# Adapter rows in column quarters, second-layer adapters through SyncE, image chunks one tile later

## The chip, the cores and the metric

One core of one Trainium2 chip runs the kernel. The metric is device time in microseconds, the median over runs of one build. TensorE is called PE here, as in the profile.

## What is computed

Two layers with a residual each, over eight sequences of 512 tokens and 2048 features, in float32. The first adds a rank-16 product, the second adds a dense product, a bias and a second rank-16 product. Which adapter (A, B pair) a sequence uses comes from two vectors of eight integers.

```python
def L0(x, A, B, ids):                       # scale 16/16 = 1
    Bx = einsum('bni,bri->bnr', x, B[ids])
    return einsum('bnr,bor->bno', Bx, A[ids])
def L1(x, ids, W, b, lora_As, lora_Bs):     # scale 32/16 = 2
    base = einsum('bti,oi->bto', x, W) + b
    h = einsum('bti,bir->btr', x, lora_As[ids])
    return base + 2 * einsum('btr,bro->bto', h, lora_Bs[ids])
x = x + L0(x, L0_A, L0_B, ids0)
x = x + L1(x, ids1, W, b, lora_As, lora_Bs)
```

## The kernel before

The dense product of 2048 by 2048 weights with two sequences at a time is cut as one level of Strassen-Winograd style blocking: `GROUPS` = 4 pairs of sequences, `PRODUCTS` = 7 block products per pair, and eight output tiles of 128 features per product. One (group, product, tile) is a **step**; there are 224, numbered `s`, and every engine walks them in the same order. A step multiplies eight 128x128 weight tiles with 128x512 tokens, each product as three matmuls of float32r halves (hi by hi, lo by hi, hi by lo; L502 to L504), so 24 matmuls. For each step SyncE (SP) loads a block of W (`w_one`, 512 KB), for products that need a sum or difference of two blocks a second (`w_two`), VectorE (DVE) sums them (L639), SP stores the sum to memory for the later groups (`w_sums`, L290), ScalarE (ACT) makes the hi half (L537), DVE the lo half (L643). A product's four pairs of x tiles go the same way (L656 or L659, L555, L665). `w_one` has three buffers, and a load into one waits until the store of its last sum has landed (L272).

Beside this runs the **background**: chunks `z`, each a 128x1024 piece that is loaded (SP, L317), split by ACT (`bg_hi`, L565) and DVE (`bg_lo`, L670) and multiplied on PE between the matmuls of a step. Chunks 0 to 31 are the **image chunks**: they carry W (`w_rows`) through the first layer's up matrices A of all eight sequences at once (L454 to L456, six matmuls a chunk), eight chunks to one column quarter j of 512 columns in `image_ps`. The last matmul of a quarter, L462, adds the two layers' rank-by-rank product (`across`) times the second layer's up rows `b1_rows`; DVE then adds the first layer's rows `a0_rows` (L781) and SP stores the quarter (L377). The finished images, one of 16 rows per sequence, are what both rank products need later. `background(s)` names the chunks of a step: steps 1 to 16 have two each. `bg_raw`, `bg_hi` and `bg_lo` have two buffers, so the load of chunk z waits until DVE has split chunk z-2, and the split of z until PE has used z-2. The SP queue is strictly in order: what stands behind such a wait waits too.

`across` needs the second layer's down matrices of all sequences (`a1_raw`), which ACT copies into contiguous columns (L607), and 16 matmuls in plain float32 (L521), which the profile counts as 32. They stand on PE between step 1 and step 2.

GpSimd (POOL) issues all loads whose address depends on an adapter number: it reads the number into a register and issues a DMA, for `a0_raw` (8 of 128 KB, L424), then `a1_raw` (8 of 128 KB, L427), then the rows: `load_rows(half)` issues 16 DMAs of 16 rows by 1024 columns (64 KB each, L415 and L417) into one buffer per table. The second half waits until quarters 0 and 1 are finished (`image_ready` 2), because it overwrites the first. Both PE (L461) and DVE (L778) wait for the whole half. Behind the rows stand POOL's loads for the later background (L392, L394) and for the ranks (L405, L407).

```python
for half in range(2):
    load_rows(half)
for s in range(STEPS):
    ...
```

## Time and profile before

| what | value |
|---|---|
| median of 3 runs | 1414.97 us (1413.96 to 1415.28) |
| the profiled execution | 1417.38 us |
| its span in the trace | 1415.7 us |
| PE busy | 1373.6 us, 97% |
| DVE busy | 939.9 us, 66% |
| ACT busy | 486.1 us, 34% |
| bytes moved by DMA | 308.38 MB, mean 218 GB/s |
| mean granted TensorE clock | 0.99 of full speed |

The page divides the span in 40 slices of 35 us. PE is at nine tenths or more in all but the first and the fifth (its digits are `3999799...`), and the granted clock dips at both places. So the question for any change is what PE waits for in the first 190 us, and the views to read are the waits by engine in a stretch of time, and the timelines of PE, POOL, ACT and DVE there. A row of a timeline gives start, duration, engine, line and shapes, with the idle time before it in brackets and what ended it.

### The profile page before, as it was taken

What the parts mean: (1) busy time and instruction counts of PE and PEld (TensorE: products, weight loads), DVE (VectorE), ACT (ScalarE), POOL (GpSimd) and SP (SyncE); (2) the same over time, 40 slices, a digit from 0 to 9 for tenths busy, and PEclk for the clock granted to TensorE, in tenths of its full rate; (3) what the DMA queues carried; (4) which work ended last, traced back from release to release, by engine and by line L of the source; (5) the groups of instructions that cost most, each with busy time, mean ns of one, the idle gap of its engine ahead of it and who ended that gap; (6) DMA issues with size and microseconds to landing.
All of it is one profiled execution on the core that took longest, in us unless ns stands there. A gap on an engine that the chain in (4) does not pass through costs nothing.

```text
span 1415.7 us, 15911 instructions
## 1 busy us (share of the span) xinstructions
PE 1373.6 (97%) x5992; PEld 1129.5 (80%) x5992; DVE 939.9 (66%) x991; ACT 486.1 (34%) x491; POOL 80.6 (6%) x166
## 2 busy tenths in 40 slices
PE   3999799999999999999999999999999999999999
PEld 2788587888887888888888888888888888888887
DVE  6587568887866665757666666566756756666662
ACT  3343244333323343433233333332223334332331
POOL 2202001001001000000101000000101000000000
PEclk8899899999999999999999999999999999999999
DMA  9999766999897444566757444556866444457642
GB/s 361 294 334 348 249 225 204 349 342 345 280 341 247 135 140 142 168 207 218 252 193 228 148 134 134 175 183 215 270 211 197 163 154 134 145 164 251 201 153 82
DMA packets 101100, 308.38 MB, mean 218 GB/s; under 512 B 13344, under 2 KB 13472, under 8 KB 101024
## 3 DMA queue, kind: packets, MB, share of 16 engines
q1 hardware_dynamic: 95328, 294.77, 62.0%
q0 software_dynamic: 5696, 12.59, 2.9%
q8 instruction: 48, 0.79, 0.2%
q14 instruction: 28, 0.23, 0.0%
HBM read 251.73 MB, written 55.57 MB: 217 GB/s over the span
## 4 chain that ended last, share of the span: by engine, by line
PE 93%; issue 3%; DMA 1%; DVE 1%; POOLq 1%; POOL 0%; ACT 0%; ACTq 0%
PE acc L502 28%; PE acc L503 28%; PE acc L504 28%; PE acc L486 2%; PE down_ps L472 2%; PE down_ps L473 2%; POOLq L386 1%; PE image_ps L456 1%; PE image_ps L455 1%; PE image_ps L454 1%; PE down_ps L521 0%; DMA a_raw<-a 0%; DMA ids_sb<-ids 0%; DMA b_rows<-b 0%; PE image_ps L462 0%
## 5 line engine op out<-in xcount | busy, mean ns | idle before, releaser
L502 PE MATMUL acc<-x_hi,w_hi 128*128 128x512 f32 x1792 | 703.6, 393 | 17.0 <-DVE x_lo L665 16.3
L503 PE MATMUL acc<-x_lo,w_hi 128*128 128x512 f32 x1792 | 699.9, 391 | 0.0
L504 PE MATMUL acc<-x_hi,w_lo 128*128 128x512 f32 x1792 | 699.3, 390 | 0.0
L537 ACT ACTIVATE w_hi<-w_one 128x1024 fp32r<-128x1024 f32 x224 | 237.5, 1060 | 679.3 <-PE acc L504 644.3
L502 PEld LDWEIGHTS acc<-x_hi,w_hi 128*128 128x128 f32 x1792 | 338.1, 189 | 91.0 <-issue 16.4
L503 PEld LDWEIGHTS acc<-x_lo,w_hi 128*128 128x128 f32 x1792 | 338.2, 189 | 72.1 <-issue 1.2
L504 PEld LDWEIGHTS acc<-x_hi,w_lo 128*128 128x128 f32 x1792 | 337.7, 188 | 71.4
L643 DVE TENSOR_TENSOR w_lo<-w_one,w_hi 128x1024 fp32r<-128x1024 f32 x224 | 273.6, 1222 | 104.2 <-ACT w_hi L537 103.9
L665 DVE TENSOR_TENSOR x_lo<-x_stage,x_hi 128x1024 fp32r<-128x1024 f32 x80 | 96.1, 1221 | 42.8 <-ACT x_hi L555 42.8
L708 DVE SCALAR_TENSOR_TENSOR sums<-acc,bias_sb,sums 128x512 f32<-128x512 f32 x128 | 95.7, 748 | 39.0 <-PE acc L486 39.0
L555 ACT ACTIVATE x_hi<-x_stage 128x1024 fp32r<-128x1024 f32 x80 | 83.5, 1056 | 110.3 <-DVE x_stage L659 82.9
L670 DVE TENSOR_TENSOR bg_lo<-bg_raw,bg_hi 128x1024 fp32r<-128x1024 f32 x64 | 77.7, 1221 | 30.5 <-ACT bg_hi L565 30.2
L565 ACT ACTIVATE bg_hi<-bg_raw 128x1024 fp32r<-128x1024 f32 x64 | 67.1, 1052 | 64.9 <-DMA bg_raw<-w_rows 35.5
L659 DVE TENSOR_TENSOR x_stage<-x_stage,resident 128x1024 f32<-128x1024 f32 x64 | 78.0, 1218 | 3.1 <-DMA x_stage<-x 3.1
L405 POOL DMA_DIRECT2D rank_raw<-images x48 | 23.4, 487 | 872.8 <-issue 872.8
L690 DVE TENSOR_TENSOR sums<-sums,acc 128x512 f32<-128x512 f32 x32 | 21.9, 685 | 64.5 <-PE acc L504 64.5
L639 DVE TENSOR_TENSOR w_one<-w_one,w_two 128x1024 f32<-128x1024 f32 x40 | 48.7, 1219 | 11.2 <-DMA w_two<-w 11.2
L472 PE MATMUL down_ps<-bg_hi,down 128*128 128x512 f32 x128 | 50.2, 392 | 1.8 <-issue 1.2
L486 PE MATMUL acc<-rank_x,rank_w 96*128 96x512 f32 x128 | 50.8, 397 | 0.0
L473 PE MATMUL down_ps<-bg_lo,down 128*128 128x512 f32 x128 | 49.8, 389 | 0.0
L687 DVE TENSOR_TENSOR sums<-sums,acc 128x512 f32<-128x512 f32 x32 | 21.9, 684 | 39.4 <-PE acc L504 39.3
L693 DVE TENSOR_TENSOR sums<-sums,acc 128x512 f32<-128x512 f32 x32 | 22.0, 686 | 39.0 <-PE acc L504 39.0
(54 smaller groups left out, 622.0 us busy)
## 6 DMA issues: line engine op xcount, KB each, us to landing
w_one<-w_sums SPq DMA_DIRECT2D x120, 512.0 KB, 3.3
w_one<-w SPq DMA_DIRECT2D x104, 512.0 KB, 5.5
x_stage<-x SPq DMA_DIRECT2D x64, 512.0 KB, 4.3
out<-sums SPq DMA_DIRECT2D x128, 256.0 KB, 4.5
w_two<-w SPq DMA_DIRECT2D x40, 512.0 KB, 8.1
w_sums<-w_one SPq DMA_DIRECT2D x40, 512.0 KB, 6.4
resident<-x SPq DMA_DIRECT2D x32, 512.0 KB, 7.4
bg_raw<-w_rows SPq DMA_DIRECT2D x32, 512.0 KB, 5.8
```

Source lines behind the costliest of these rows:

```text
L472: pe.matmul(down_ps[:, :], weights, hi[:, u, :], start=(c == 0), stop=False)
L473: mm = pe.matmul(down_ps[:, :], weights, lo[:, u, :], start=False, stop=(c == C - 1))
L486: pe.matmul(acc[s % BANKS][:, :], rank_w[:, P * o:P * (o + 1)], rank_x[side][:, :], start=False, stop=True, skip_group_check=True).then_in ...
L502: pe.matmul(ps[:, :], w_hi[ws][:, c, :], hi, start=(c == 0), stop=False)
L503: pe.matmul(ps[:, :], w_hi[ws][:, c, :], lo, start=False, stop=False)
L504: mm = pe.matmul(ps[:, :], w_lo[ws][:, c, :], hi, start=False, stop=(c == H - 1))
L537: act.activation(w_hi[s % W_PARTS][:, :, :], w_one[s % W_ONES][:, :, :], ACT.Copy).then_inc(w_hi_ready, 1)
L555: act.activation(x_hi[q % X_PARTS][:, :, :], x_source(p, r), ACT.Copy).then_inc(x_hi_ready, 1)
L643: dve.tensor_tensor(w_lo[s % W_PARTS][:, :, :], w_one[s % W_ONES][:, :, :], f32(w_hi[s % W_PARTS][:, :, :]), ALU.subtract).then_inc(w_read ...
L659: dve.tensor_tensor(stage, stage, resident[1 if i in (2, 6) else 0][:, cs, :], ALU.subtract if i in (1, 6) else ALU.add).then_inc(x_summed, 1)
L665: dve.tensor_tensor(x_lo[q % X_PARTS][:, :, :], x_source(p, r), f32(x_hi[q % X_PARTS][:, :, :]), ALU.subtract).then_inc(x_ready, 1)
L708: dve.scalar_tensor_tensor(out=tile, in0=acc[s % BANKS][:, :], scalar=bias_sb[:, f:f + 1], in1=tile, op0=ALU.add, op1=ALU.add).then_inc(ba ...
```

## The change

- The rows come by quarter: `load_rows(j)` for j = 0 to 3 issues 16 DMAs of 16 rows by 512 columns (32 KB each), `b1` ahead of `a0`, into buffer j % 2 with a semaphore of its own. Quarters 2 and 3 wait for quarter 0 and 1 (`image_ready` 1 and 2). There are 64 such DMAs in place of 32, with the same bytes.
- The eight `a1_raw` loads leave POOL. SP reads the numbers and issues them, behind the loads for step 2 and ahead of `mask`, `bias` and the first store of a sum.
- Image chunks begin in step 2, not 1: two a step, three in steps 11 and 14, the last still in step 16. Chunks 0 and 1 go from ahead of `across` to behind it on PE, ACT, DVE and SP.
- DVE makes the first lo half of x before the second sum of x, not after it.

On PE, before: the end of step 1 (`acc` is the dense product, `image_ps` the image, `down_ps` here the matmuls of `across`).

```order
L504 MATMUL acc<-x_hi,w_lo 128x512
L454 MATMUL image_ps<-bg_hi,a_hi 128x512
L455 MATMUL image_ps<-bg_hi,a_lo 128x512
L456 MATMUL image_ps<-bg_lo,a_hi 128x512
L454 MATMUL image_ps<-bg_hi,a_hi 128x512
L455 MATMUL image_ps<-bg_hi,a_lo 128x512
L456 MATMUL image_ps<-bg_lo,a_hi 128x512
L502 MATMUL acc<-x_hi,w_hi 128x512
L503 MATMUL acc<-x_lo,w_hi 128x512
L504 MATMUL acc<-x_hi,w_lo 128x512
L502 MATMUL acc<-x_hi,w_hi 128x512
L503 MATMUL acc<-x_lo,w_hi 128x512
```

And after, from the end of step 1 on:

```order
L507 MATMUL acc<-x_lo,w_hi 128x512
L508 MATMUL acc<-x_hi,w_lo 128x512
L527 MATMUL down_ps<-a_raw,sums 128x128 x16
L506 MATMUL acc<-x_hi,w_hi 128x512
L507 MATMUL acc<-x_lo,w_hi 128x512
L508 MATMUL acc<-x_hi,w_lo 128x512
L506 MATMUL acc<-x_hi,w_hi 128x512
L507 MATMUL acc<-x_lo,w_hi 128x512
L508 MATMUL acc<-x_hi,w_lo 128x512
L458 MATMUL image_ps<-bg_hi,a_hi 128x512
L459 MATMUL image_ps<-bg_hi,a_lo 128x512
L460 MATMUL image_ps<-bg_lo,a_hi 128x512
```

Step 1 now has no image matmul in it; the first stands behind `across` and six matmuls of step 2.

On SP, before: the start of the queue.

```order
L296 DMA resident<-x 128x1024 x8
L279 DMA w_one<-w 128x1024
L284 DMA w_two<-w 128x1024
L317 DMA bg_raw<-w_rows 128x1024 x2
L279 DMA w_one<-w 128x1024
L284 DMA w_two<-w 128x1024 [waits w_summed]
L352 DMA mask_sb<-mask 128x128
L353 DMA bias_sb<-bias 128x16
L290 DMA w_sums<-w_one 128x1024 [waits w_summed] x2
L279 DMA w_one<-w 128x1024 [waits w_kept0,w_ready]
L284 DMA w_two<-w 128x1024 [waits w_summed]
L306 DMA x_stage<-x 128x1024 [waits x_ready]
```

And after, in two places:

```order
L280 DMA w_one<-w 128x1024
L285 DMA w_two<-w 128x1024 [waits w_summed]
L346 TENSOR_LOAD ids_sb [waits ids_loaded]
L346 ISA x2
L357 ISA
L357 DMA a_raw<-a 128x256
```

```order
L359 DMA mask_sb<-mask 128x128
L360 DMA bias_sb<-bias 128x16
L291 DMA w_sums<-w_one 128x1024 [waits w_summed] x2
L280 DMA w_one<-w 128x1024 [waits w_kept0,w_ready]
L285 DMA w_two<-w 128x1024 [waits w_summed]
L307 DMA x_stage<-x 128x1024 [waits x_ready]
L318 DMA bg_raw<-w_rows 128x1024 x2
```

The first two chunk loads (1 MB) left the place ahead of step 2's weights and stand behind step 3's; the eight adapter loads (1 MB) came in behind step 2's weights.

```diff
--- before.py
+++ after.py
@@ -69,8 +69,9 @@
     if g:
         places = (0, 2, 4, 5)
         return [IMAGE + 16 * g + 4 * i + places.index(o)] if i < 4 and o in places else []
-    if 1 <= s <= 16:
-        return [2 * s - 2, 2 * s - 1]
+    if 2 <= s <= 16:
+        first = 2 * (s - 2) + (s > 11) + (s > 14)
+        return list(range(first, first + (3 if s in (11, 14) else 2)))
     if 19 <= s <= 22:
         return [IMAGE + 2 * (s - 19), IMAGE + 2 * (s - 19) + 1]
     return [IMAGE + 8 + s - 24] if 24 <= s <= 31 else []
@@ -165,8 +166,8 @@
             sb("first_tiles", [P, 2, T], F32, early)
             a0_hi = sb("a0_hi", [P, C, NB, R], F32R, early)
             a0_lo = sb("a0_lo", [P, C, NB, R], F32R, early)
-            a0_rows = sb("a0_rows", [P, D // 2], F32, early)
-            b1_rows = sb("b1_rows", [P, D // 2], F32, early)
+            a0_rows = [sb(f"a0_rows{k}", [P, T], F32, early) for k in range(2)]
+            b1_rows = [sb(f"b1_rows{k}", [P, T], F32, early) for k in range(2)]
             image = sb("image", [P, T], F32, early)
             mask_sb = sb("mask_sb", [P, P], F32, early)
             across = sb("across", [P, P], F32, early)
@@ -194,7 +195,7 @@
         a0_loaded = sem("a0_loaded")
         a1_loaded = sem("a1_loaded")
         mask_loaded = sem("mask_loaded")
-        rows_loaded = sem("rows_loaded")
+        rows_loaded = [sem(f"rows_loaded{k}") for k in range(2)]
         a1_ready = sem("a1_ready")
         across_done = sem("across_done")
         across_ready = sem("across_ready")
@@ -341,14 +342,20 @@
                 sp.dma_start(out[C * (2 * g + side) + H * half + o], sums[(2, 1, 2, 0)[i - 3]][:, o, :])\
                   .then_inc(out_stored[o], DMA)
 
+            def adapter(n, table):
+                a = sp.value_load(ids_sb[0:1, 1, n:n + 1], min_val=0, max_val=table.shape[0] - 1)
+                return table[bass.ds(a, 1)]
+
             load_w(0)
             for r in range(CH):
                 for k in range(2):
                     load_resident(0, k, r)
             load_w(1)
-            for z in background(1):
-                load_bg(z)
             load_w(2)
+            sp.wait_ge(ids_loaded, 2 * DMA)
+            for n in range(NB):
+                sp.dma_start(a1_raw[:, n, :, :], adapter(n, a1).rearrange("u p c r -> (u p) c r"))\
+                  .then_inc(a1_loaded, DMA)
             sp.dma_start(mask_sb[:, :], mask).then_inc(mask_loaded, DMA)
             sp.dma_start(bias_sb[:, :], bias).then_inc(bias_loaded, DMA)
             keep_sum(0)
@@ -406,16 +413,16 @@
                         .then_inc(rank_loaded, DMA)
                     pool.dma_start(rank_raw[row + R:row + 2 * R, :], up).then_inc(rank_loaded, DMA)
 
-            def load_rows(half):
-                if half:
-                    pool.wait_ge(image_ready, 2)
-                cols = slice(D // 2 * half, D // 2 * (half + 1))
+            def load_rows(j):
+                if j >= 2:
+                    pool.wait_ge(image_ready, j - 1)
+                cols = slice(T * j, T * (j + 1))
                 for n in range(NB):
                     rows = slice(R * n, R * (n + 1))
-                    pool.dma_start(a0_rows[rows, :], adapter(0, n, a0).rearrange("u r d -> (u r) d")[:, cols])\
-                        .then_inc(rows_loaded, DMA)
-                    pool.dma_start(b1_rows[rows, :], adapter(1, n, b1).rearrange("u r d -> (u r) d")[:, cols])\
-                        .then_inc(rows_loaded, DMA)
+                    pool.dma_start(b1_rows[j % 2][rows, :], adapter(1, n, b1).rearrange("u r d -> (u r) d")[:, cols])\
+                        .then_inc(rows_loaded[j % 2], DMA)
+                    pool.dma_start(a0_rows[j % 2][rows, :], adapter(0, n, a0).rearrange("u r d -> (u r) d")[:, cols])\
+                        .then_inc(rows_loaded[j % 2], DMA)
 
             pool.dma_start(ids_sb[:, 0, :], ids0).then_inc(ids_loaded, DMA)
             pool.dma_start(ids_sb[:, 1, :], ids1).then_inc(ids_loaded, DMA)
@@ -423,11 +430,8 @@
             for n in range(NB):
                 pool.dma_start(a0_raw[:, n, :, :], adapter(0, n, a0_down).rearrange("u p c r -> (u p) c r"))\
                     .then_inc(a0_loaded, DMA)
-            for n in range(NB):
-                pool.dma_start(a1_raw[:, n, :, :], adapter(1, n, a1).rearrange("u p c r -> (u p) c r"))\
-                    .then_inc(a1_loaded, DMA)
-            for half in range(2):
-                load_rows(half)
+            for j in range(4):
+                load_rows(j)
             for s in range(STEPS):
                 g, i, o = where(s)
                 if s + 4 in FIRST:
@@ -458,8 +462,8 @@
                     if k == 7:
 
                         pe.wait_ge(across_ready, 1)
-                        pe.wait_ge(rows_loaded, 2 * NB * DMA * (j // 2 + 1))
-                        pe.matmul(ps[:, :], across[:, :], b1_rows[:, T * (j % 2):T * (j % 2 + 1)],
+                        pe.wait_ge(rows_loaded[j % 2], 2 * NB * DMA * (j // 2 + 1))
+                        pe.matmul(ps[:, :], across[:, :], b1_rows[j % 2][:, :],
                                   start=False, stop=True).then_inc(image_done, 1)
                     return
                 if k == 0:
@@ -512,6 +516,8 @@
                         add_rank(s - 1)
                     if c == 5 and len(zs) > 1:
                         multiply_chunk(zs[1])
+                    if c == 6 and len(zs) > 2:
+                        multiply_chunk(zs[2])
 
             step(0)
             step(1)
@@ -601,8 +607,6 @@
             act.wait_ge(a0_loaded, NB * DMA)
             act.activation(a0_hi[:, :, :, :], a0_raw[:, :, :, :].rearrange("p n c r -> p c n r"), ACT.Copy)\
                .then_inc(a0_hi_ready, 1)
-            for z in background(1):
-                split_bg(z)
             act.wait_ge(a1_loaded, NB * DMA)
             act.activation(a1_cols.rearrange("p (c n r) -> p c n r", c=C, n=NB),
                            a1_raw[:, :, :, :].rearrange("p n c r -> p c n r"), ACT.Copy).then_inc(a1_ready, 1)
@@ -732,8 +736,8 @@
             sum_w(0)
             sum_x(0, 0)
             split_w(0)
+            split_x(0, 0)
             sum_x(0, 1)
-            split_x(0, 0)
             sum_x(0, 2)
             split_x(0, 1)
             sum_x(0, 3)
@@ -746,8 +750,6 @@
             dve.tensor_tensor(a0_lo[:, :, :, :], a0_raw[:, :, :, :].rearrange("p n c r -> p c n r"),
                               f32(a0_hi[:, :, :, :]), ALU.subtract).then_inc(a0_ready, 1)
             sum_w(2)
-            for z in background(1):
-                split_bg(z)
             for s in range(STEPS):
                 g, i, o = where(s)
                 p = PRODUCTS * g + i
@@ -775,11 +777,11 @@
                 if s - 1 in IMAGE_LAST:
                     j = IMAGE_LAST[s - 1]
                     dve.wait_ge(image_done, j + 1)
-                    dve.wait_ge(rows_loaded, 2 * NB * DMA * (j // 2 + 1))
+                    dve.wait_ge(rows_loaded[j % 2], 2 * NB * DMA * (j // 2 + 1))
                     if j:
                         dve.wait_ge(image_stored, DMA * j)
-                    dve.tensor_tensor(image[:, :], image_ps[j % 2][:, :], a0_rows[:, T * (j % 2):T * (j % 2 + 1)],
-                                      ALU.add).then_inc(image_ready, 1)
+                    dve.tensor_tensor(image[:, :], image_ps[j % 2][:, :], a0_rows[j % 2][:, :], ALU.add)\
+                       .then_inc(image_ready, 1)
                 if s - 1 in LAST:
                     split_rank_x(LAST[s - 1])
                 if s + 1 in FIRST:
```

## Rows read from the trace of the kernel before

**Rows 1.** The page: its first line and the busy time of PE.

```profile
span 1415.7 us, 15911 instructions
...
PE 1373.6 (97%) x5992; PEld 1129.5 (80%) x5992; DVE 939.9 (66%) x991; ACT 486.1 (34%) x491; POOL 80.6 (6%) x166
```

**Rows 2.** Busy time by stretch: stretch, length, PE, PEld, DVE, ACT, POOL, clock, DMA share, GB/s.

```profile
240.00:1416.00 1176.00, 1170.11 (x5141) 964.81 (x5139) 778.24 (x829) 392.21 (x398) 49.82 (x102) 1.00 0.61 203
...
154.00:155.00 1.00, 1.00 (x3) 0.35 (x2) 0.00 (x0) 0.00 (x0) 0.00 (x0) 0.50 0.94 307
```

**Rows 3.** Waits from 0 to 60 us: engine and line, releaser, total us, times, longest.

```profile
PE down_ps L521 <- ACT sums L607: 3.3, 1, 3.3
...
DVE x_stage L656 <- DMA resident<-x: 4.0, 4, 1.7
```

**Rows 4.** Waits from 60 to 240 us.

```profile
PE image_ps L462 <- DMA b_rows<-b: 10.6, 1, 10.6
```

**Rows 5.** Timeline of PE, steps 1 and 2.

```profile
25.84 0.50 PE L502 MATMUL acc<-x_hi,w_hi 128*128 128x512 f32 x1
...
33.53 0.80 PE L454 MATMUL image_ps<-bg_hi,a_hi 128*128 128x512 f32 x1 [6.04 <-DVE bg_lo L670]
...
46.12 6.56 PE L521 MATMUL down_ps<-a_raw,sums 128*128 128x128 f32 x32 [3.33 <-ACT sums L607]
...
52.43 0.48 PE L502 MATMUL acc<-x_hi,w_hi 128*128 128x512 f32 x1
```

**Rows 6.** Timeline of POOL and ACT in the first 50 us.

```profile
26.97 1.91 ACT L602 ACTIVATE a_hi<-a_raw 128x2048 fp32r<-128x2048 f32 x1 [2.45 <-DMA a_raw<-a_down]
...
37.73 0.54 POOL L427 DMA_DIRECT2D a_raw<-a  x1 [6.14 <-issue]
...
44.07 1.91 ACT L607 ACTIVATE sums<-a_raw 128x2048 f32<-128x2048 f32 x1 [13.29 <-DMA a_raw<-a]
```

**Rows 7.** Timeline of the SP queue, first 31 us.

```profile
10.27 4.33 SPq L353 DMA_DIRECT2D bias_sb<-bias  x1
...
30.20 0.43 SPq L306 DMA_DIRECT2D x_stage<-x  x1
```

**Rows 8.** DMA issues from 0 to 60 us: KB each, us to landing.

```profile
bias_sb<-bias SPq DMA_DIRECT2D x1, 8.0 KB, 17.9
```

**Rows 9.** Timeline of POOL, the second half of the rows.

```profile
122.69 0.49 POOL L415 DMA_DIRECT2D a_rows<-a  x1 [64.32 <-issue]
...
148.68 0.48 POOL L417 DMA_DIRECT2D b_rows<-b  x1 [6.94 <-issue]
```

**Rows 10.** Timeline of PE around the long wait.

```profile
153.54 2.04 PE L462 MATMUL image_ps<-b_rows,across 128*128 128x512 f32 x2 [10.58 <-DMA b_rows<-b]
...
157.83 0.40 PE L502 MATMUL acc<-x_hi,w_hi 128*128 128x512 f32 x1
```

**Rows 11.** Timeline of DVE and PE: chunks 4, 6, 8, 20, 22; PE uses 20.

```profile
58.45 1.22 DVE L670 TENSOR_TENSOR bg_lo<-bg_raw,bg_hi 128x1024 fp32r<-128x1024 f32 x1
...
66.11 1.23 DVE L670 TENSOR_TENSOR bg_lo<-bg_raw,bg_hi 128x1024 fp32r<-128x1024 f32 x1 [0.50 <-ACT bg_hi L565]
...
76.97 2.35 DVE L670 TENSOR_TENSOR bg_lo<-bg_raw,bg_hi 128x1024 fp32r<-128x1024 f32 x2
...
127.75 2.35 DVE L670 TENSOR_TENSOR bg_lo<-bg_raw,bg_hi 128x1024 fp32r<-128x1024 f32 x2
...
129.18 0.39 PE L454 MATMUL image_ps<-bg_hi,a_hi 128*128 128x512 f32 x1
...
135.64 1.23 DVE L670 TENSOR_TENSOR bg_lo<-bg_raw,bg_hi 128x1024 fp32r<-128x1024 f32 x1 [1.77 <-ACT bg_hi L565]
```

**Rows 12.** DMA from 52 to 142 us: SP's queue, chunk loads.

```profile
q1 hardware_dynamic: 8128, 29.09, 93.0%
...
bg_raw<-w_rows SPq DMA_DIRECT2D x20, 512.0 KB, 5.9
```

**Rows 13.** Timeline of PE, the first matmul of step 17.

```profile
191.41 0.39 PE L502 MATMUL acc<-x_hi,w_hi 128*128 128x512 f32 x1
```

## What the change does to the time: the prediction

> **What bounds the kernel now.** I read the page first. PE is busy 1373.6 of 1415.7 us [rows 1]; only 42 us are left to any change that keeps the matmuls, as this one does. The busy time by stretch says where: from 240 us to the end PE works 1170.11 of 1176 us at full clock [rows 2]. So the end of the kernel is set by PE, and whatever PE wins before 240 us comes through whole, if the later stage keeps its relative order. The change touches nothing after step 17, except that POOL's loads come earlier. From that stretch I also take PE's pace: 1170.11 us / 5141 matmuls = 0.228 us each; below I use 0.227.
>
> Next I read the waits of PE and the timelines around them. There are two places. The first is steps 1 and 2. Step 1 starts at 25.84, does six matmuls, then stands 6.04 us for the lo half of chunk 0 [rows 5]. After the step PE waits 3.3 us more for ACT's copy of the second layer's matrices [rows 3], does the 32 pieces of `across` in 6.3 us (46.12 to 52.43) and starts step 2 at 52.43 [rows 5]. The cause of the 3.3 stands on POOL and ACT: the last adapter load of the second layer is issued at 37.73 after a hole of 6.14 us, and ACT waits 13.29 us until 44.07 [rows 6]. The second place is the long wait: PE stands 10.58 us, until 153.54, for the rows of the second half [rows 4, 10]. POOL could begin them only at 122.69, when quarter 1 was finished, and issues one every 1.14 us or so; the sixteenth fell on a hole of 6.94 us and left at 148.68 [rows 9].
>
> **The sum, part by part.** All times are of the profiled execution (1417.38 us; 2.4 above the median 1414.97).
>
> *Chunks 0 and 1 out of step 1.* Step 1 still starts at 25.84, since what released it is w_lo, which is not moved. Its 24 matmuls then run through: 25.84 + 24 x 0.227 = 31.3.
>
> *Adapters on SP.* In SP's queue, in order, 8.4 MB stand ahead of the last adapter load: weights and x for steps 0 to 2 (7.3 MB) and the adapters themselves (1.05 MB). Before, exactly as much stood ahead of `bias`, with two chunk loads in the adapters' place. It was issued at 10.27 and landed 17.9 us later, at 28.2 [rows 7, 8]. So I put the adapters' landing at 28.2. SP's eight register reads and issues, at POOL's 1.14 us, take until 18 us, which the queue's backlog hides. The 4.33 us that `bias` took to issue [rows 7] says SP was held back by a full queue anyway. ACT finishes the first layer's split at 26.97 + 1.91 = 28.9 [rows 6] and copies the second's until 30.8, ahead of 31.3. The 3.3 us wait is gone.
>
> *`across` itself.* It took 6.3 us at, nearly throughout, the lower clock, because PE had just stood. Now PE comes from step 1 without a hole. No row shows it at the higher clock. Bounds: 6.3 us, and half of it, 3.2; I take 3.7, near the low end, since the dense matmuls go from 0.427 to 0.227 when the clock rises. Step 2 starts at 31.3 + 3.7 = 35.0. It started at 52.43 with 12 chunk matmuls already done, which now follow: 12 x 0.227 = 2.7. **Gain 52.4 - 35.0 - 2.7 = 14.7 us** (12.1 with the slow `across`).
>
> *The rows by quarter.* Quarter 2 needs only quarter 0's buffer. POOL can issue its 16 DMAs at some 80 us, 18 us of issuing, one hole of 7 and 5 of landing: ready by 110, while PE asks for it in step 13, near 137. Quarter 3: released near 112, ready by 142, asked for near 160. So the 10.58 us wait goes, and with it the lower clock behind it (0.50 at 154 us, [rows 2]). Between 153.54 and 157.83 PE does L462 (two pieces) and six matmuls in 4.3 us; at full clock they take 2.2. **Gain 10.6 + 2.1 = 12.7 us.** The 32 extra issues cost POOL 36 us. I cost them at nothing: POOL's next work, the loads for chunk 32 on, is needed after step 17. Without that cover they would cost their length past it.
>
> *First lo half of x earlier.* PE starts some 1.4 us earlier, but the later pairs wait for the loads of x [rows 3], which do not move. Between 0 and 1.4 us I take 0, as the last pair decides.
>
> Sum so far: 27.4 us. The block of steps up to the end of step 16 would end at 191.4 [rows 13] - 27.4 = 164.0.
>
> *What is late next: the chunks.* They are now asked for 15 to 27 us earlier, and the last 14 in six steps. Three prices. (1) Chunk 0 is loaded behind step 3's first x_stage, at 30.20 + 0.43 [rows 7] = 30.6; with 5.9 us to landing [rows 12], ACT 1.06 and DVE 1.22, it is ready at 38.9, and PE wants it at 35.0 + 6 x 0.227 = 36.4: 2.5 us of waiting, 0 to 2.1 more if the clock falls (the excess of [rows 10]); 3.5. (2) Before, DMA was already full from 52 to 142 us (SP's queue alone held 93% of the engines' time, [rows 12]), and the chunks lost their lead: from chunk 4 to chunk 22 DVE's start went from 58.45 to 135.64, 8.58 us a pair, where PE takes 36 x 0.227 = 8.2. Chunk 20's lo half was done only some 0.3 us before its use (127.75 + 1.22, used 129.18, [rows 11]). With no lead to start from, 0.4 a pair over eight pairs is 3 us. (3) In steps 11 to 16 PE asks for a pair every 7.7 us. At 8.58 that is 0.9 x 7 = 6 more; but half of these steps have light weight traffic, so the chunks can come faster: 1 to 2. Sum 8, of bounds 1 (the queue gains what PE gives it) and 12. Check from the other end: 38.9 + 15.5 pairs x 8.58 = 171.9, and 3.6 us of matmuls behind the last chunk: 175.5, so 11.5 late is the full price of a chain that never catches up.
>
> **Forecast: 27.4 - 8 = 19.4, with rounding 20 us**, 1397.4 in a profiled execution, 1395 as a median.
>
> **Rivals.**
> - *Full gain.* Chunks arrive faster because DMA has no gap before step 2 any more. For it: the engines' share falls when PE is slow, so capacity is left there. Against: the shrinking lead of [rows 11]. Only price (1) at its least: saves 26, 1389. Chance 0.16.
> - *Adapters late on SP.* One queue in order is slower for them than POOL's own. For it: loads of the same time landed 17.9 us after issue on SP [rows 8], and eight reads and issues stand ahead of the sum's store, for which step 3's weights wait. If they land 6 us later than 28.2, PE stands 5 us, the clock falls, `across` takes 6.3: step 2 starts near 42.5, and chunk 0's wait is covered. Saves 27.4 - 7.5 - 4.5 = 15, 1400. Chance 0.18. The Trainium skill (DMA: Bandwidth & Descriptors, "Queues, rings and completion order") says each DMA engine goes round-robin between the queues it has work for, packet by packet, and consumes one queue in order; by that rule a load moved from POOL's queue behind SP's backlog loses its turn, which speaks for this rival. The trace agrees with the rule so far (POOL's last adapter load, issued at 37.73, was in by 44.07, [rows 6], beside SP's 17.9), but the bytes ahead say 28.2.
> - *Three chunks starve.* In steps 11 and 14 the third chunk needs its buffer, freed only in the step before, and SP stands behind that wait, so the weights of two steps on are late too. Each costs 3 to 5 us with the clock's fall: 8 on top, saves 11.5, 1403.5. For it: chunk 20's 0.3 us. Chance 0.12.
> - *A hole remains.* POOL's holes fall elsewhere and a quarter is still late, or the change does not remove the long wait: saves 14.7 less 7, 1407. Against: 27 us of margin for quarter 2, 18 for quarter 3. Chance 0.03.
> - *Slower.* The chain load, ACT, DVE becomes PE's bound over the whole block because 64 small DMAs and the adapters disturb it. Place: steps 2 to 16. Price: the slowest pair before took 10.9 us (66.11 to 76.97, [rows 11]). At that pace the block ends at 38.9 + 15.5 x 10.9 + 3.6 = 211.5, 20 us later than now: 1435. It decides from 191.4 = 42.5 + 15.5p, p = 9.6 us a pair. Against: the mean is 8.58. Chance 0.03. The Trainium skill (same page, the section "Measured (HBM→SBUF, 128 partitions, SWDGE, issued from GpSimd)") calls transfers under 64 KB descriptor-dominated, and the row loads go from 64 to 32 KB; it would speak for this rival, but they are 2.1 MB in all.
>
> **How the numbers follow.** The forecast has 0.48: 1391 to 1399. I can tell from no change about 0.2%, 2.8 us. Every case but the last is faster by more: 0.95 faster, 0.02 the same, 0.03 slower. The range takes in full gain (1388) and the starved steps (1405).
>
> **What would show it.** In the trace after: step 2's first matmul near 35; `across` in some 3.7 us at clock 1.0; no wait at L466 of microseconds; adapters' copy starting at 28.9; a wait of 2 to 3 us for chunk 0; short waits of PE for `bg_lo` in steps 9 to 15; step 17 starting near 172. A copy that starts past 31 makes the second rival right, PE never waiting for `bg_lo` the first. If PE after 240 us is less than 99% busy, my premise that the rest is untouched is wrong.

## The result, and the profile after

| | before | after |
|---|---|---|
| median of 8 runs each | 1413.95 us (1412.76 to 1415.54) | 1409.57 us (1405.57 to 1411.68) |
| profiled execution, its span | 1417.38, 1415.7 us | 1411.09, 1409.2 us |

The ratio is 0.9962, with a 95% interval of 0.9951 to 0.9973: faster by 5.4 us of 1415 (4.4 by the medians), where 20 were forecast. 1409.57 lies outside the range of the prediction, on its slow side.

The page of the kernel after: span, busy times, the shares by engine of the chain that ends last, and the cost of making the chunks' hi halves on ACT.

```profile
span 1409.2 us, 16105 instructions
PE 1374.2 (98%) x5992; PEld 1127.3 (80%) x5992; DVE 940.1 (67%) x991; ACT 485.7 (34%) x491; POOL 91.7 (7%) x190
...
PE 84%; DMA 7%; DVE 4%; SPq 2%; ACT 1%; issue 1%; DVEq 0%; ACTq 0%
...
L571 ACT ACTIVATE bg_hi<-bg_raw 128x1024 fp32r<-128x1024 f32 x64 | 67.3, 1054 | 82.8 <-DMA bg_raw<-w_rows 72.3
```

PE does the same work as in [rows 1]. The other two lines tell where to look. The chain that sets the end was 93% PE in the page of before; here it is 84%, and 7% is DMA. ACT's idle time ahead of `bg_hi` that a chunk's load ended was 35.5 us and is 72.3.

Busy time of the kernel after by stretch (columns as in [rows 2]): the late stage, two stretches of the chunk stage, and the five microseconds behind chunk 0.

```profile
240.00:1409.00 1169.00, 1164.81 (x5121) 961.52 (x5119) 772.46 (x823) 390.67 (x396) 46.91 (x96) 1.00 0.61 203
41.00:46.00 5.00, 4.94 (x12) 3.88 (x13) 4.36 (x6) 1.56 (x2) 1.94 (x4) 0.50 1.04 354
60.00:152.00 92.00, 84.15 (x358) 66.32 (x357) 69.18 (x68) 35.18 (x35) 16.23 (x34) 1.00 0.93 325
152.00:186.00 34.00, 31.75 (x129) 24.90 (x128) 18.52 (x19) 12.16 (x12) 1.38 (x3) 0.95 0.70 226
```

After 240 us PE is busy 99.6% of the time, as in [rows 2]: the late stage is untouched. Between 60 and 152 us PE now stands 8 of 92 us; the kernel before was busy 82.00 of 82.00 from 60 to 142. From 152 to 186 it loses time and some of the clock (0.95).

The timeline of PE in the kernel after, at the places of [rows 5], and its start of step 17.

```profile
31.76 3.73 PE L527 MATMUL down_ps<-a_raw,sums 128*128 128x128 f32 x32
35.25 0.48 PE L506 MATMUL acc<-x_hi,w_hi 128*128 128x512 f32 x1
...
41.06 0.79 PE L458 MATMUL image_ps<-bg_hi,a_hi 128*128 128x512 f32 x1 [4.20 <-DVE bg_lo L674]
...
185.80 0.39 PE L506 MATMUL acc<-x_hi,w_hi 128*128 128x512 f32 x1
```

Step 1 (from 26.26) runs through, `across` stands behind it without a wait and takes 3.73 us, step 2 starts at 35.25, where it started at 52.43. Of that only 5.6 us are left when step 17 starts (185.80, [rows 13] had 191.41). The waits of PE from 60 to 240 us:

```profile
PE image_ps L458 <- DVE bg_lo L674: 10.0, 8, 2.4
...
PE acc L506 <- DVE w_lo L647: 0.5, 1, 0.5
```

The one long wait for the rows [rows 4] has gone, and eight short ones for a chunk's lo half came. DVE waited for ACT there, and ACT for the load:

```profile
ACT bg_hi L571 <- DMA bg_raw<-w_rows: 59.9, 25, 7.7
DVE bg_lo L674 <- ACT bg_hi L571: 31.1, 20, 4.7
```

Putting the first image matmul of some chunks side by side shows the pattern (us; the step in brackets):

| chunk | before | after |
|---|---|---|
| 2 | 53.91 (2) | 51.89 (3) |
| 8 | 79.31 (5) | 78.96 (6) |
| 15 | 107.87 (8) | 107.52 (9) |
| 23 | 141.45 (12) | 146.61 (13) |
| 31 | 187.80 (16) | 182.18 (16) |

At chunk 8 and at chunk 15 both kernels are at the same absolute time. What the change won shows only as one more step (24 dense matmuls, 5.5 us) done beside them. The 28.6 us between these two chunks are PE's own pace in both (126 matmuls of 0.227), so what the kernel after loses in the first half it loses ahead of chunk 8. From chunk 16 on the kernel after is slower than the chunks' old pace. So two theories stood against each other.

- **Supply**: the chain load, ACT, DVE for the chunks, through SP's queue in order and two buffers, is what sets the time of this stage, whatever PE wins ahead of it.
- **Arrangement**: the loss is made by something the change itself put there: chunk 0 loaded late, three chunks in steps 11 and 14, or the adapters in SP's queue.

### The profile page after: what moved, and what is told of

It is laid out like the page before. It is cut to its first block, busy times and chain, and to the rows that moved or that the text cites. A ratio compares the mean times of both kernels' runs of the same rounds, so it can differ in the third digit from the quotient of the medians.

```text
span 1409.2 us, 16105 instructions
## 1 busy us (share of the span) xinstructions
PE 1374.2 (98%) x5992; PEld 1127.3 (80%) x5992; DVE 940.1 (67%) x991; ACT 485.7 (34%) x491; POOL 91.7 (7%) x190
## 4 chain that ended last, share of the span: by engine, by line
PE 84%; DMA 7%; DVE 4%; SPq 2%; ACT 1%; issue 1%; DVEq 0%; ACTq 0%
PE acc L506 26%; PE acc L507 26%; PE acc L508 26%; DMA bg_raw<-w_rows 6%; PE down_ps L476 2%; PE acc L490 2%; PE down_ps L477 2%; DVE bg_lo L674 1%; ACT bg_hi L571 1%; DMA w_two<-w 1%; DVE w_one L643 1%; DMA w_sums<-w_one 1%; SPq L357 0%; DVE w_lo L647 0%; SPq L297 0%
## 5 line engine op out<-in xcount | busy, mean ns | idle before, releaser
L571 ACT ACTIVATE bg_hi<-bg_raw 128x1024 fp32r<-128x1024 f32 x64 | 67.3, 1054 | 82.8 <-DMA bg_raw<-w_rows 72.3
L697 DVE TENSOR_TENSOR sums<-sums,acc 128x512 f32<-128x512 f32 x32 | 22.0, 686 | 38.9 <-PE acc L508 38.9
```

Of the source, the lines that this page charges most:

```text
L571: act.activation(bg_hi[z % 2][:, :, :], bg_source(z), ACT.Copy).then_inc(bg_hi_ready, 1)
```

## The experiments

Every ratio below is to the kernel before in the same session, whose median was 1415.2 to 1415.9 us there. `A` marks an edit to the kernel after, `B` one to the kernel before. "Version 2" is the kernel of experiment 2, and so on. The expectations call some of them by other names: e1 is experiment 1, e2 is 3, e3 is 6, e7 is 2.

### 1. Two chunks a step (A)

```diff
-    if 2 <= s <= 16:
-        first = 2 * (s - 2) + (s > 11) + (s > 14)
-        return list(range(first, first + (3 if s in (11, 14) else 2)))
+    if 2 <= s <= 17:
+        return [2 * (s - 2), 2 * (s - 2) + 1]
```

> The changed kernel with two image chunks in every step from 2 to 17, none with three; the last quarter is finished one step later. Theory A (the steps with three chunks are at fault: SP stands behind the third chunk's wait and the next steps' weights and chunks are late): of the 11.4 us that chunks 18 to 31 came late, 8 to 11 are saved, so some 1400 us, and PE's waits for the lo halves after chunk 18 nearly vanish. Theory B (the DMA engines are simply full and every byte has its price): the same bytes must arrive before the same work, so 1408 to 1411, with the waits spread evenly over the steps. Theory C (the last quarter finished later pushes the rank work): a new wait of PE around step 24, 1412 or more.

Measured: 1409.63 us, ratio 0.9961 (0.9947 to 0.9974): nothing gained on the median. Yet the trace shows chunk 31 at 177.76, in step 17. Less the 5.5 us of one more step's dense matmuls that is 172.3, 9.9 us ahead of the kernel after. That is Theory A's 8 to 11 us. Part of it was lost again right behind. The SP queue of this kernel, and PE at step 19:

```profile
166.73 0.43 SPq L279 DMA_DIRECT2D w_one<-w  x1
180.17 0.33 SPq L327 DMA_DIRECT2D sums<-x  x1
180.54 0.43 SPq L279 DMA_DIRECT2D w_one<-w  x1
181.02 0.90 SPq L317 DMA_DIRECT2D bg_raw<-x  x2
```

```profile
191.99 0.47 PE L475 MATMUL down_ps<-bg_hi,down 128*128 128x512 f32 x1 [3.64 <-DVE down L717]
```

SP issues nothing for 13 us: the load of x into `sums` for step 18 waits until the fourth quarter is finished, which now happens a step later. I had not seen this wait. SP stands there in the kernels before and after too (11 to 12 us), but PE waits for nothing behind it: from step 18 to step 24 both take 40.0 us, this version 43.8, version 2 of the next experiment 40.6. In the trace this version is still 6.1 us ahead of the kernel after at step 24 (225.21 to 231.29). The profiled execution (1406.82) was the fastest of six, up to 1411.97, and why the median kept none of the 6 us no run shows.

### 2. The same, with that load behind the chunk loads of the next iteration (A)

```diff
-                if s + 2 < STEPS:
-                    load_sum(s + 2)
+                for t in {16: [], 17: [18, 19]}.get(s, [s + 2]):
+                    if t < STEPS:
+                        load_sum(t)
```

> Two chunks a step in steps 2 to 17, and SP's load of the running sum of step 18 moved behind the chunk loads of the next iteration, so that SP does not stand until the last quarter is done. In e1 that stand delayed chunks 32 and 33 and with them PE by 3.6 us and 2 us of lower clock. If e1 had won step 17's dense work and lost it there: 5 us below e1, 1402 to 1405. If the supply of chunks gives no gain from more room: 1408 to 1410.

Measured: 1402.37 us, ratio 0.9910 (0.9892 to 0.9928), chunk 31 at 177.87. That is in the range of the first case. This version is 7.4 us ahead of the kernel after (0.9962 less 0.9910, of 1415). The late load of `sums` only takes back the stand of experiment 1; in the kernel after PE lost nothing to it. What three chunks in a step do is plain in the two SP queues. After:

```profile
114.05 9.60 SPq L318 DMA_DIRECT2D bg_raw<-w_rows  x3
123.69 0.43 SPq L291 DMA_DIRECT2D w_sums<-w_one  x1
...
146.58 9.48 SPq L318 DMA_DIRECT2D bg_raw<-w_rows  x3
```

And with two a step:

```profile
112.93 2.19 SPq L317 DMA_DIRECT2D bg_raw<-w_rows  x2
115.17 0.43 SPq L290 DMA_DIRECT2D w_sums<-w_one  x1
115.69 0.38 SPq L279 DMA_DIRECT2D w_one<-w  x1
116.11 0.89 SPq L284 DMA_DIRECT2D w_two<-w  x1
```

The third load needs the buffer of the first, which DVE splits only in its next iteration (two splits from 122.07 on); SP stands until 123.65, and the store of a sum, the weights and the next chunks stand behind it. The busy time by stretch, 119 to 124 us, after and with two a step:

```profile
119.00:124.00 5.00, 4.19 (x19) 3.17 (x18) 4.21 (x4) 2.88 (x3) 0.00 (x0) 1.00 0.11 44
```

```profile
119.00:124.00 5.00, 4.10 (x18) 3.11 (x17) 5.00 (x6) 3.04 (x3) 0.00 (x0) 1.00 0.92 342
```

The DMA engines run nearly empty (a share of 0.11, 44 GB/s) in the stage that lives on them; with two a step it is 0.92 and 342 GB/s. No run kept three chunks in a step and moved the third load alone, so the runs show what 15 steps in place of 16 cost, and the traces show the stand. At chunk 23, between the two steps with three, version 2 is 5.1 us ahead (144.19, less half a step's 2.7, to 146.61), at chunk 31 9.8: each such step cost some 5 us.

### 3. Chunks 0 and 1 loaded earlier (A)

The two loads go from behind step 3's weights to directly behind the adapters, ahead of `mask` (20.28 us in place of 31.41).

```diff
                   .then_inc(a1_loaded, DMA)
+            for z in background(2):
+                load_bg(z)
             sp.dma_start(mask_sb[:, :], mask).then_inc(mask_loaded, DMA)
...
-                for z in background(s + 2):
-                    load_bg(z)
+                if s:
+                    for z in background(s + 2):
+                        load_bg(z)
```

> The changed kernel with the loads of chunks 0 and 1 issued behind the adapters and ahead of the mask, not behind step 3's weights. If chunk 0's late load is a cost of its own, the 4.2 us wait at 41 us and the 2.4 us of lower clock behind it go: 1402 to 1404 us. If the chain of chunks is bound by DMA throughput from there on, the lateness only moves to the next chunks: 1408 to 1410 us.

Measured: 1409.34 us, 0.9956 (0.9943 to 0.9968), not to be told from the kernel after, as in the second case of the expectation. Chunk 0's first matmul is at 41.02, where it was at 41.06. DVE tells why:

```profile
38.60 1.23 DVE L646 TENSOR_TENSOR w_one<-w_one,w_two 128x1024 f32<-128x1024 f32 x1 [3.61 <-DMA w_two<-w]
39.75 2.35 DVE L677 TENSOR_TENSOR bg_lo<-bg_raw,bg_hi 128x1024 fp32r<-128x1024 f32 x2
```

The data was there, but the split stands in DVE's order behind the sum of step 3's weights, whose load came 3 us later now. One megabyte sooner was another megabyte later.

### 4. Loads earlier and DVE's splits ahead of that sum, on top of experiment 2 (A)

```diff
-                if s:
+                if s == 1:
+                    for z in background(2):
+                        split_bg(z)
+                    sum_w(3)
+                elif s:
```

> The kernel of e7, with the loads of chunks 0 and 1 behind the adapters (as in e2) and, on DVE, their lo halves ahead of the sum of step 3's weights, on which they stood in e2 until 38.6 us. If the chain's start decides: chunk 0 is ready by 36 us, chunk 2 some 4 us earlier than 51.8, no wait and no lower clock at 36 to 46: 5 to 7 us below e7, 1396 to 1399. If DMA throughput has taken over by then: the same as e7.

Measured: 1404.94 us, 0.9920 (0.9903 to 0.9937); 2.6 us worse than experiment 2 by the median, with intervals that overlap. The 5 to 7 us of gain did not come. Chunk 0 came at 36.2 as wished. Then chunk 2 came at 52.05, and PE stood 7.5 us for it: its load, issued at 36.85 behind the weights of two steps, let ACT start at 49.68. A wait taken away at chunk 0 came back, larger, at chunk 2.

### 5. Half of the bytes (A)

Chunks 2 to 31 load 128x512 of 128x1024, so the images are not the reference's; every instruction and wait stays.

```diff
+                if 2 <= z < IMAGE:
+                    sp.dma_start(bg_raw[y % 2][:, 0:1, :], source[:, 0:1, :]).then_inc(bg_loaded[y % 2], DMA)
+                    return
```

> The changed kernel, but of the image chunks from number 2 on only the first 512 of 1024 columns per partition are loaded (256 KB each, 30 of them, 7.9 MB less); the other half of each chunk buffer keeps old numbers, so the images are not the reference's. ACT, DVE and PE work as before. Theory S1 (the time to bring a chunk's bytes through the full DMA queue paces the chunks): the chunks come at PE's pace, the waits after chunk 1 vanish, some 14 us less: 1395 to 1398. Theory S2 (the chain's own steps, two buffers and the order of SP's queue pace them, whatever their bytes): 1407 to 1410.

Measured: 1399.94 us, 0.9897 (0.9877 to 0.9917): 9.2 us ahead of the kernel after, between the two theories and nearer S1 (1395 to 1398). Chunk 31 came at 170.21. So the bytes in the queue carry much of the loss, but the run does not tell how much of its gain is the three-chunk steps' of experiment 2, whose third load is shorter here too, so the two sizes are not to be added.

### 6. Rows by quarter alone (B)

```diff
-            for half in range(2):
-                load_rows(half)
+            for j in range(4):
+                load_rows(j)
```

(with the two buffers, the two semaphores and the new `load_rows`; nothing else of the change.)

> The kernel before with only the rows by quarter: SP, the adapters and the chunks stay as they were. The long wait of 10.6 us and 2.1 us of lower clock go. If nothing is given back: 1401 us. If the chunks, whose lead was down to some 0.3 us, become PE's bound for chunks 24 to 31 as in the changed kernel, 3 to 6 us are given back: 1404 to 1407 us. If POOL's earlier issues disturb the start, more.

Measured: 1405.72 us, 0.9932 (0.9920 to 0.9945): 9.6 us less than before, and less than the whole change takes. It is the second case: PE now waits 0.8 us for chunk 20 and 1.0 for chunk 24, where it waited for neither.

### 7. The other parts without it: rows by half (A)

> The changed kernel with the rows by half again. The long wait comes back at the end of quarter 2, since POOL may begin the second half only when quarter 1 is finished. By the trace after that is at 131 us and 32 us later the rows are there, 13 to 15 us after PE asks. The chunks use that wait to get ahead, so their 8 us of lateness behind it go: 1414 to 1417 us, which would say that the change's early part alone is worth nothing. If early part and rows add up (each worth what it showed), 1414 us as well but with PE's chunk waits of steps 14 and 15 unchanged.

Measured: 1420.58 us, 1.0037 (1.0025 to 1.0049). The adapters on SP and the later chunks alone make the kernel slower by 5.2 us, more than either case said. The waits of PE, from 60 to 240 us:

```profile
PE image_ps L466 <- DMA b_rows<-b: 8.9, 1, 8.9
PE image_ps L458 <- DVE bg_lo L674: 6.1, 5, 3.9
```

Ahead of them PE stands 7.5 us for chunk 0, until 43.89, where the kernel after stands 4.2, until 41.06. The only edit is in the rows.

### 8. Adapters on SP alone (B)

```diff
-            for n in range(NB):
-                pool.dma_start(a1_raw[:, n, :, :], adapter(1, n, a1).rearrange("u p c r -> (u p) c r"))\
-                    .then_inc(a1_loaded, DMA)
...
+            sp.wait_ge(ids_loaded, 2 * DMA)
+            for n in range(NB):
+                sp.dma_start(a1_raw[:, n, :, :], adapter(n, a1).rearrange("u p c r -> (u p) c r"))\
+                  .then_inc(a1_loaded, DMA)
```

> The kernel before with one part alone: the second layer's adapters loaded by SyncE (and the first lo half of x earlier); rows by half and the chunks as before. Theory (parts add up where PE waits for a load by itself, and the chunks had a head start to live on): this part alone takes away the 3.3 us wait for the copied matrices and gives across at full clock, about 6 us; since rows by quarter alone gave 9.5 and both together 14.4, I expect 14.4 - 9.5 = 4.9 us less than before, 1409 to 1411. Rival (the chunks set the time up to the long wait, whatever comes ahead of them): under 2 us, since chunk 16 reaches DVE at the same time as before and quarter 1 ends no earlier, 1413 to 1415.

Measured: 1414.01 us, 0.9988 (0.9979 to 0.9997); the rival was right, 1.7 us. PE in this kernel:

```profile
41.60 3.73 PE L528 MATMUL down_ps<-a_raw,sums 128*128 128x128 f32 x32
...
49.79 0.76 PE L459 MATMUL image_ps<-bg_hi,a_hi 128*128 128x512 f32 x1 [3.06 <-DVE bg_lo L677]
```

```profile
151.72 2.04 PE L467 MATMUL image_ps<-b_rows,across 128*128 128x512 f32 x2 [11.16 <-DMA b_rows<-b]
```

`across` starts 4.5 us earlier than in [rows 5] and takes 2.8 us less. A wait of 3.06 for chunk 2 comes at once, and chunk 15 is only 2.4 us earlier (105.49, before 107.87). POOL starts the second half of the rows at 120.30, 2.4 earlier too, and the long wait ends at 151.72, 1.8 ahead of [rows 10], which is the whole gain. PE had won 7 us at step 2; the chunks let 2.4 of it through, and the wait for the rows 1.8.

### 9. Adapters on SP and rows by quarter, chunks as before (A)

```diff
-    if 2 <= s <= 16:
-        first = 2 * (s - 2) + (s > 11) + (s > 14)
-        return list(range(first, first + (3 if s in (11, 14) else 2)))
+    if 1 <= s <= 16:
+        return [2 * s - 2, 2 * s - 1]
```

(with the loads and splits of chunks 0 and 1 back at their old places on SP, ACT and DVE.)

> The changed kernel with only its third part undone: chunks in steps 1 to 16, two a step, loaded and split as in the kernel before; rows by quarter and adapters through SP stay. Supply theory (the chunk chain decides, and starting it later than need be costs what it wins elsewhere): PE waits at 27 to 33 us as before, then across follows step 1 at full clock near 46, and everything up to chunk 22 comes 6 us earlier than in e3: 1399 to 1402. If the chunks are paced by DMA throughput from the start, whatever the order: as e3, 1404 to 1407.

Measured: **1401.10 us, 0.9899 (0.9880 to 0.9917)**: 14.3 us less than before, 8.9 less than the kernel after, and ahead of both. From 0 to 60 us PE waits 6.3 us for chunk 0, and from 60 to 240 us:

```profile
PE image_ps L459 <- DVE bg_lo L677: 1.1, 2, 0.8
PE down_ps L477 <- DVE bg_lo L677: 0.6, 1, 0.6
PE acc L507 <- DVE w_lo L650: 0.5, 1, 0.5
```

Supply theory's range (1399 to 1402) holds. The two parts are worth more together (14.3) than apart (9.6 and 1.7), and the difference arises ahead of the long wait: at chunk 15 this version is at 101.58, version 8 at 105.49, the kernel with the rows alone at 107.99 (before: 107.87). POOL issues all 16 DMAs of 64 KB, 1 MB, from 22.67 to 40.00 in version 8, and half of these bytes in that time here. The sum of weights that stands ahead of chunk 2's split starts on DVE at 42.28 there and at 38.26 here. So the adapters' win gets past chunk 2 with the smaller rows beside it. That the rows' bytes in the full queue make the difference is likely, with chunk 0 in experiment 7 as a second case, but no run changed them alone at this place.

### 10. Version 9 with half of the bytes

> The version with the adapters on SyncE, rows by quarter and chunks in steps 1 to 16 (1401.1), in which chunks 2 to 31 load half of their bytes, so that their images are not the reference's. Theory (a full SyncE queue paces the chunks, and in this version they have a head start that just covers it): PE waits for chunks only for 1.1 us after chunk 0, so at most 3 us are gained, 1398 to 1400, with chunk 31 near 168.5. Rival (the transfers' pace costs in every version alike, for PE also waits for other things that stand in that queue): as much as the change gained from it, 9 to 10 us, 1391 to 1392.

Measured: 1397.65 us, 0.9873 (0.9858 to 0.9888), 3.7 less than version 9 by the ratios, whose intervals just overlap; chunk 31 at 168.62, where version 9 has 170.42. The theory stands: with two chunks a step this half of the chunks' bytes costs a few microseconds, not nine.

### 11. The old places of the loads, the new places on PE

Experiment 2 with chunks 0 and 1 loaded ahead of step 2's weights and split as before, and 2 and 3 one iteration earlier.

> PE takes two chunks a step in steps 2 to 17, as in the version with the late load of the sums (1402.4), but the loads keep their old places: chunks 0 and 1 ahead of step 2's weights, 2 and 3 one iteration earlier, and ACT and DVE split 0 and 1 at their old place. Theory (the lost head start is what the later beginning costs): chunk 0 waits for nothing (splits end near 33.5, PE asks at 37), chunks run one tile behind PE's demand with slack, so step 2 starts near 36 and the end comes 3 to 6 us ahead of the version with chunks in steps 1 to 16: 1395 to 1398. Rival (the queue only holds what it holds; a tile's delay on PE moves the chain's buffers too, so loads from chunk 4 on start later and the lead is gone by chunk 8): 1400 to 1403, no better than 1401.1.

Measured: 1404.46 us, 0.9925 (0.9912 to 0.9939). The rival was nearer, and my theory of a lost head start fell. Chunk 0 (38.37) waits for nothing; then PE stands 5.1 us for chunk 2, until 51.80. DVE at that place:

```profile
49.38 1.23 DVE L647 TENSOR_TENSOR w_one<-w_one,w_two 128x1024 f32<-128x1024 f32 x1 [3.32 <-DMA w_two<-w]
50.53 2.36 DVE L678 TENSOR_TENSOR bg_lo<-bg_raw,bg_hi 128x1024 fp32r<-128x1024 f32 x2
```

ACT had made both hi halves by 46.7. The lo halves stood behind the sum of step 4's weights, issued at 37.13 and landed at 49.3: in a full queue another load was late, and DVE's fixed order made it chunk 2's.

### 12. Version 9, with chunks 0 and 1 between `across` and step 2 on PE alone

```diff
-                zs = background(s)
+                zs = background(s) if s != 1 else []
...
             mm.then_inc(across_done, 1)
+            for z in background(1):
+                multiply_chunk(z)
```

> The version with the chunks as before (1401.1) with one edit on PE alone: chunks 0 and 1 are multiplied between across and step 2, not inside step 1. Step 1 then runs through to 31.5, across waits 1.4 us for ACT's copy, and step 2 starts near 39.7 where it started at 46.06, so PE has 6.4 us in hand at once, with loads and splits in their old places. Theory (from chunk 2 on the supply sets the time; what PE wins ahead of it is mostly lost again): PE waits for chunk 2, for DVE splits it behind a sum of weights whose load is late, until near 43, and again here and there on the way; chunk 31 comes at 168 to 170, of the 6.4 us 0 to 2.5 come through: 1398.5 to 1401.5. Rival (the version with the chunks as before had slack in its supply, and only PE's own waits counted): 5 to 6.4 come through, 1395 to 1396.

Measured: 1400.92 us, 0.9901 (0.9885 to 0.9918), the same as version 9. The rows of PE:

```profile
33.31 3.81 PE L528 MATMUL down_ps<-a_raw,sums 128*128 128x128 f32 x32 [1.50 <-ACT sums L616]
...
39.73 0.39 PE L507 MATMUL acc<-x_hi,w_hi 128*128 128x512 f32 x1
...
44.82 0.50 PE L459 MATMUL image_ps<-bg_hi,a_hi 128*128 128x512 f32 x1 [3.58 <-DVE bg_lo L679]
```

Step 2 starts at 39.73, 6.3 us ahead of version 9's 46.06. At chunk 2 PE is 2.7 us ahead (44.82 to 47.53), at chunk 15 level (101.66 to 101.58), at chunk 31 0.8 us behind (171.21 to 170.42). All 6.3 us are gone, 5.4 of them by chunk 3 (50.66 to 51.63). This is the plainest case for **supply**: one edit on PE, everything else in place.

Chunks 15 and 31 in all versions with the adapters on SP, the rows by quarter and all bytes, less 5.5 us where the chunk sits a step later:

| version | chunk 15 | chunk 31 | ratio |
|---|---|---|---|
| after | 102.0 | 182.2 (as it is) | 0.9962 |
| 3 (chunks 0 and 1 loaded earlier) | 101.9 | 182.1 (as it is) | 0.9956 |
| 1 (two a step) | 102.1 | 172.3 | 0.9961 |
| 2 (two a step, late sum) | 101.6 | 172.4 | 0.9910 |
| 4 (loads and splits earlier) | 102.3 | 174.8 | 0.9920 |
| 11 (old places of the loads) | 102.5 | 173.2 | 0.9925 |
| 9 (chunks as before) | 101.6 | 170.4 | 0.9899 |
| 12 (PE's order alone) | 101.7 | 171.2 | 0.9901 |

At chunk 15 all agree within 1 us, the kernel after among them, however they began. Behind it the two with three chunks in a step lose some 10 us. So both theories hold, each at its place: supply eats what is won at the head of the stage, and the arrangement costs 10 us behind chunk 15.

## Why the prediction was wrong

**What held.** Step 1 starts at 26.26 (said: 25.84) and runs through; the adapters are there when ACT wants them, and the copy starts at 29.26 (said: 28.9); `across` takes 3.49 us from its start to step 2's (said: 3.7); step 2 starts at 35.25 (said: 35.0). The bytes ahead in the queue were the right measure: the adapters landed 12.1 us after issue (median), and all were in by 29.26 (said: 28.2). The rival of late adapters cost PE nothing here. It leaned on what the Trainium skill says of DMA engines that take turns between queues (DMA: Bandwidth & Descriptors, "Queues, rings and completion order"). The trace fits it: from 9 to 21 us loads of the same 128 KB on POOL's own queue landed 5.7 us after issue (median), less than half of SP's 12.1. The wait for the rows went as said, and the 32 extra issues of POOL cost nothing: quarter 3's last left at 151.77, and PE used the quarter at 183.54. By itself that part gave 9.6 us (experiment 6) of the 12.7 of its term.

**What failed** is the term "What is late next: the chunks". I priced it at 8, of bounds 1 and 12. Step 17 started at 185.80 where the sum without that term says 164.0: 21.8. Some 9.4 of it were lost up to chunk 15 and 12.4 behind it. Even the check from the other end, a chain that never catches up (175.5), was 10 us too early.

- *Price (3), three chunks in steps 11 and 14, is the step that was wrong.* I took 1 to 2 us, because "the chunks can come faster" there. I compared rates only, and did not follow the third load through the queue: it needs a buffer that DVE frees one iteration later, and everything of SP stands behind it. In the trace two a step bring chunk 31 9.8 us earlier (172.4 to 182.2), by the ratios version 2 is 7.4 us ahead; it still loses some 4 us of PE's pace behind chunk 15 itself. I had it among the rivals, at the right place and at 8 us, and gave it 0.12. Even that rival (1403.5) was 6 us too fast, since the other prices were too low as well.
- *Prices (1) and (2)* were 6.5 together. Up to chunk 15 they were some 9: chunk 15 would come at 98.1 with step 2 at 35.0, 36 matmuls of 0.227 a step and the two of L466, and came at 107.52. The larger part is price (1), put at 3.5: chunk 0 was to be ready at 38.9 and was ready at 41.0, PE stood 4.2 us for it, and its next 12 matmuls took 5.2 us at the lower clock, where 2.7 are due, so it was 6.7. The pairs' pace, price (2), took some 2 by chunk 15. But price (1) was no cost of chunk 0 alone. Experiments 3, 4, 11 and 12 show a stiffer thing: whichever place these loads have, and whatever PE wins, chunk 15 comes at the same time, and what is taken away at chunk 0 comes back at chunk 2.
- *The sum itself was the wrong form.* It adds PE's gains ahead of the stage and subtracts a fee. In a stage where another chain sets the time, the gains ahead are worth what reaches the chain, as in experiment 8 (7 us at step 2, 1.7 at the end) and 12 (6.3 and 0). I had the row that says so, the lead of chunk 20, and drew from it a fee. By [rows 11] that lead is 0.2 us (128.97 to 129.18), not the 0.3 that I wrote. The rival of full gain is off as well: with price (1) at its least, 2.5, the sum saves 24.9, not 26.

**Where the time went**, by ratio times 1415 us: adapters and rows -14.3 (version 9); the chunks one tile later with two a step and the late load of `sums`, +1.6, inside the uncertainty (version 2); 32 chunks in 15 steps in place of 16, +7.4 (the kernel after). The sum is -5.3, and measured was -5.4. The saving of the first two parts was real; the third part gave most of it back.

**What stays open.** How the cost of the head of the block, the 3.6 to 7.5 us that PE stands for chunk 0 or chunk 2 in every version with both good parts, could be had is not settled: no order that I tried made both come in time. Nor is it shown which of the loads in the full queue would have to go; of halving the chunks' own bytes version 9 gains some 2 us in the trace. A third buffer for the chunks was not tried.

## What to carry to other kernels

When a stage is fed by a queue in strict order, follow one piece through it, buffer by buffer, before pricing a new schedule: here a load that waited for a buffer of the same iteration stopped everything behind it, and emptied the transfer engines in the stage that needed them most. Time won ahead of a chain that already binds is worth only what reaches the chain's end; the sign is a lead that shrinks to tenths of a microsecond. Try each part of a change alone and one left out: here the two good parts are worth 14.3 us without the third and 5.4 with it.

## What the runs showed of the hardware

- SP's eight register reads and loads of the adapters took from 9.13 to 20.64 us, 1.44 us each, while POOL's row loads left every 1.13 us or so. The shortest of the eight issues took 0.34 us, the longest 2.48. That points to SP being held back by its full queue, as with `bias` in [rows 7], but no run took the queue's load away to show it:

```profile
9.13 11.51 SPq L357 DMA_DIRECT2D a_raw<-a  x8
20.68 1.01 SPq L359 DMA_DIRECT2D mask_sb<-mask  x1
```

- The granted clock followed some stands of PE and not others. After 4.20 us without work it was 0.50 from 41 to 46 us. In version 12, after a stand of 3.58, it was still full for 2 us and then 0.72 on average over the next 6. In the kernel after, the six waits of 0.6 to 2.4 us between 60 and 152 us left it at 1.00, on the mean of that stretch, and yet the wait of 1.91 us before 168.17 was followed by a mean of 0.70 from 170 to 174 us. The rows are of version 12:

```profile
44.00:46.00 2.00, 1.18 (x5) 0.99 (x6) 1.43 (x2) 1.75 (x2) 0.97 (x2) 1.00 1.05 400
46.00:52.00 6.00, 6.00 (x21) 4.76 (x20) 4.87 (x6) 1.32 (x2) 2.32 (x5) 0.72 1.03 336
```

- A transfer of 512 KB for step 4's weights took 12 us from issue to use in version 11 (37.13 to 49.3), beside a median of 9.0 and a least of 5.4 for the `w_two` loads from 20 to 60 us there: with the queue full, the time of issue alone says little of the landing.
